# Four taps to a transpose instead of three in a two-block deformable-convolution kernel

## What is computed

```python
acc = acc + wgt[:, None] * g          # four corners of the bilinear sample, per tap
z = jnp.einsum('bckhw,ock->bohw', cols, w.reshape(O, C, 9))
...
x = x + L0(_gn(x))                    # one deformable convolution, relu
x = x + L1(_gn(x))                    # two of them, batch norm and gelu, own residual
```

## Time and profile before

| | us |
|---|---|
| median of 3 runs | 6690.79 (6690.13 to 6698.08) |
| the profiled execution, first to last instruction | 6690.3 |
| PE busy | 6000.0 (90%) |
| PE loading weights | 4792.9 (72%) |
| DVE busy | 4534.0 (68%) |
| POOL busy | 4608.7 (69%) |
| ACT busy | 2208.6 (33%) |

### The profile page before, as it was taken

How to read it: one execution, slowest core, us unless ns; L and a number is a source line. 1 busy time by engine, 2 the same in 40 slices (tenths; PEclk the granted TensorE clock), 3 DMA queues, 4 the chain that set the end, 5 groups by cost and what they waited for, 6 DMA issues and landing times. The chain is left out here.

```text
span 6690.3 us, 124828 instructions
## 1 busy us (share of the span) xinstructions
PE 6000.0 (90%) x48293; PEld 4792.9 (72%) x48293; DVE 4534.0 (68%) x8624; ACT 2208.6 (33%) x3376; POOL 4608.7 (69%) x4765
## 2 busy tenths in 40 slices
PE   6997998987988988998987998899989989998996
PEld 6886777766777767777765666677767777776775
DVE  6886776856777856777754555477667767676675
ACT  1222222232222222222322222244434444443442
POOL 0005777766777767777777777777777777777776
PEclk9998999988999988999987898899989999998998
DMA  5334344435343433444422332333333334333333
GB/s 148 99 99 116 100 112 114 113 88 141 100 112 104 119 82 108 109 111 107 110 79 75 82 78 73 98 87 84 84 94 95 91 80 103 91 88 86 87 84 77
DMA packets 505472, 653.42 MB, mean 98 GB/s; under 512 B 116137, under 2 KB 412121, under 8 KB 496985
## 3 DMA queue, kind: packets, MB, share of 16 engines
q0 software_dynamic: 152064, 311.73, 18.8%
q1 hardware_dynamic: 352856, 333.94, 17.7%
HBM read 599.16 MB, written 46.15 MB: 96 GB/s over the span
## 5 line engine op out<-in xcount | busy, mean ns | idle before, releaser
L895 POOL DMA_INDIRECT G<-table,IDX x4752 | 4594.6, 967 | 2036.7 <-issue 1932.9
L2282 DVE TENSOR_TENSOR ARENA<-ARENA,OUT 128x864 f32<-128x864 f32 x936 | 937.5, 1048 | 142.7 <-PE RED L1123 94.7
L1517 ACT ACTIVATE SAMP<-RED 96x384 f32<-96x384 f32 x688 | 335.2, 487 | 1889.8 <-PE RED L1335 824.9
L1123 PE MATMUL RED<-IDENT,ARENA 128*96 128x128 f32 x7344 | 876.1, 279 | 73.0 <-DVE ARENA L2282 73.0
L2085 DVE TENSOR_TENSOR G<-G,WPS 128x1152 f32<-128x1152 f32 x528 | 711.1, 1347 | 309.3 <-DMA G<-table,IDX 308.0
L1123 PEld LDWEIGHTS RED<-IDENT,ARENA 128*96 128x96 f32 x7344 | 816.5, 129 | 117.4 <-issue 114.3
L1316 PE MATMUL BTP<-PAD,ARENA 80*128 x2304 | 748.5, 448 | 56.8 <-DVE ARENA L2078 29.9
L1072 PE MATMUL OFF<-PAD,ARENA 128*54 128x128 f32 (+1 forms) x10944 | 748.5, 295 | 12.7 <-ACT PAD L1417 6.8
L1072 PEld LDWEIGHTS OFF<-PAD,ARENA 128*54 128x54 f32 (+1 forms) x10944 | 666.9, 134 | 112.9 <-issue 97.5
L1196 PE MATMUL BTP<-X 80*128 80x480 f32 x1248 | 648.7, 638 | 105.8 <-ACT X L1461 57.0
L1512 ACT ACTIVATE SAMP<-RED 96x384 f32<-96x384 f32 x528 | 257.3, 487 | 1450.4 <-PE RED L1138 733.7
(11 more groups left out here) (216 smaller groups left out, 7777.7 us busy)
## 6 DMA issues: line engine op xcount, KB each, us to landing
ARENA<-wtab SPq DMA_DIRECT2D x416, 400.0 KB
G<-table,IDX POOLq DMA_INDIRECT x4752
ARENA<-xo SPq DMA_DIRECT2D x96, 720.0 KB
X<-xo SPq DMA_DIRECT2D x80, 360.0 KB, 3.8
table<-TB SPq DMA_DIRECT2D x64, 384.0 KB, 2.5
X<-x SPq DMA_DIRECT2D x3, 3200.0 KB, 18.2
out<-X SPq DMA_DIRECT2D x20, 320.0 KB
wtab<-TB SPq DMA_DIRECT2D x16, 384.0 KB, 3.1
```

Of the source, the lines that this page charges most:

```text
L895: pool.indirect_dma_start(G[:, b, k, :], None, tables[seg.table], bass.IndirectOffsetOnAxis(ap=IDX[:, q, b * TAPS + k:b * TAPS + k + 1], a ...
L1123: last = nc.tensor.matmul(RED[b % 2][0:TPG * C, gr * 128:(gr + 1) * 128], PROD[gr][:, sft, :], IDENT[:, :], start=(sft == 0), stop=(sft == ...
L1517: nc.scalar.activation(SAMP[:, x], RED[x][0:TPG * C, 0:GROUPS * 128].rearrange("p (g n) -> p g n", g=GROUPS), ACT.Copy).then_inc(z.samp_re ...
L2282: nc.vector.tensor_tensor(out=PROD[gr].rearrange("p (dy dx) (j c) -> p j dy dx c", dy=3, j=TPG), in0=win.rearrange("p j dy (dx c) -> p j d ...
```

## The change

`TPB = 4`: taps go to transposes in blocks of four, four and one. A block of four fills 128 columns.

- Dense: `PROD` becomes one buffer for eight taps, nine shifts, and `PROD8` one for the ninth tap. PE makes 9 transposes for taps 0 to 3, 9 for taps 4 to 7, and 3 for the last tap: four shifts, one shift, four shifts at a time. These last leave four partial sums on the partitions, and the projection adds them, with the last tap's weights present four times in `WDCN`. 21 transposes a unit instead of 27.
- DVE still works dense taps by threes, but the third group is split in two taps (576 elements) and one (288). So PE's first block waits for two DVE instructions (`prod` counts 4 a unit now, 16 a tile) and DVE's second instruction waits for PE's second block of the unit before.
- Strips: 10, 10 and 3 transposes (23 instead of 30 a unit), DVE's instructions stay, one per tap.
- Gathered tiles: as many transposes as before, with 128, 128 and 32 columns instead of 96 each. Half strips stay at three groups, with their own weights `WHALF`.
- Start: `WDCN` is loaded by 24 DMAs and `WHALF` by one, all behind the two loads of `X`, where three DMAs stood ahead of them; PE waits for them before its first work (`norm`, k = 0). DVE clears both `RED` banks first.
- Smaller: ACT copies 128 instead of 96 partitions; `PRODS`, `OFFX`, `PXP` move.

```diff
-        PROD = [arena(5468 + 864 * i, 864).rearrange("p (s c) -> p s c", s=9) for i in range(GROUPS)]
+        PROD = arena(5468, 9 * 2 * TPB * C).rearrange("p (s k c) -> p s k c", s=9, k=2 * TPB)
+        PROD8 = arena(5468 + 9 * 2 * TPB * C, 9 * C).rearrange("p (s k c) -> p s k c", s=9, k=1)
...
-                sp.dma_start(WDCN[:, s], w_dcn[s]).then_inc(consts_loaded, 16)
             for h in range(HALVES):
                 load_x(h).then_inc(x_loaded, 16)
+            for s in (L0, C1, C2):
+                for k, n in ((0, 3), (3, 1), (4, 2), (6, 2)):
+                    at, src = k % TPB * C, k % TPG * C
+                    sp.dma_start(WDCN[at:at + n * C, s, k // TPB, :], w_dcn[s][src:src + n * C, k // TPG, :]).then_inc(wdcn_loaded, 16)
+                for r in range(TPB):
+                    sp.dma_start(WDCN[r * C:(r + 1) * C, s, 2, :], w_dcn[s][2 * C:3 * C, 2, :]).then_inc(wdcn_loaded, 16)
+            sp.dma_start(WHALF[:, :, :], w_dcn[C1]).then_inc(wdcn_loaded, 16)
...
+            def sum_window(red, gr):
+                if gr < GROUPS - 1:
+                    for sft in range(9):
+                        last = nc.tensor.matmul(red[:, gr * 128:(gr + 1) * 128], PROD[:, sft, TPB * gr:TPB * (gr + 1), :].rearrange("p k c -> p (k c)"),
+                                                IDENT[:, :], start=(sft == 0), stop=(sft == 8), is_transpose=True)
+                    return last
+                for sft, n in ((0, 4), (8, 1), (4, 4)):
+                    last = nc.tensor.matmul(red[0:n * C, gr * 128:(gr + 1) * 128], PROD8[:, sft:sft + n, 0, :].rearrange("p s c -> p (s c)"),
+                                            IDENT[:, :], start=(sft == 0), stop=(sft == 4), is_transpose=True)
+                return last
...
                 def norm(k, h, half, src, u=None, z=main):
                     pe.wait_ge(normed_s, k + 1)
                     pe.wait_ge(normed_v, k + 1)
+                    if k == 0:
+                        pe.wait_ge(wdcn_loaded, 16 * NWDCN)
...
                         for gr in range(GROUPS):
-                            pe.wait_ge(prod, 12 * step.i + 3 * b + gr + 1)
-                            for sft in range(9):
-                                last = nc.tensor.matmul(RED[b % 2][0:TPG * C, gr * 128:(gr + 1) * 128],
-                                                        PROD[gr][:, sft, :], IDENT[:, :],
-                                                        start=(sft == 0), stop=(sft == 8), is_transpose=True)
-                            last.then_inc(prod_used, 1)
+                            pe.wait_ge(prod, 16 * step.i + 4 * b + gr + 2)
+                            sum_window(RED[b % 2], gr).then_inc(prod_used, 1)
...
-                    pe.wait_ge(weighted, 36 * (now.s.first + now.k) + 9 * b + 3 * gr + 3)
+                    pe.wait_ge(weighted, 36 * (now.s.first + now.k) + 9 * b + min(TPB * (gr + 1), TAPS))
...
                 def weight_window(step, b, gr):
-                    dve.wait_ge(prod_used, step.wg + (GROUPS if step.drain and b == 0 else 3 * b + gr + 1))
+                    dve.wait_ge(prod_used, step.wg + (GROUPS if step.drain and b == 0 else 3 * b + min(gr + 1, 2)))
+                    if gr < GROUPS - 1:
+                        on.weight_taps(step, b, gr, 0, TPG, PROD[:, :, TPG * gr:TPG * (gr + 1), :])
+                        return
+                    on.weight_taps(step, b, gr, 0, 2, PROD[:, :, TPG * gr:TPG * gr + 2, :])
+                    dve.wait_ge(prod_used, step.wg + (GROUPS if step.drain and b == 0 else 3 * b + 3))
+                    on.weight_taps(step, b, gr, 2, 1, PROD8)
```

More of the change, by code:

```diff
@@ L13 @@
 TAPS, GROUPS, TPG = 9, 3, 3
+TPB = 4
 PW = W + 2
@@ L184, in build_program @@
         SHIFT = arena(7078, 1)
-        PXP = spare(1576, 256, 1)
+        PXP = ARENA[0:1, 6208:6464]
         IOTA = sb("IOTA", [128, WY])[:, :]
@@ L932, in _, with turn_taps, sum_rows @@
         def _(pe):
+            def turn_taps(red, b):
+                for gr in range(GROUPS):
+                    taps_ = SUM[:, b % 2, TPB * gr:min(TPB * (gr + 1), TAPS), :].rearrange("p k c -> p (k c)")
+                    last = nc.tensor.transpose(red[0:taps_.shape[1], gr * 128:(gr + 1) * 128], taps_, IDENT[:, :])
+                return last
[8 more added lines that the diff above has]
+                                            IDENT[:, :], start=(sft == 0), stop=(sft == 4), is_transpose=True)
+                return last
+            def sum_rows(red, gr):
+                if gr < GROUPS - 1:
+                    for w in range(WY):
+                        last = nc.tensor.matmul(red[:, gr * 128:(gr + 1) * 128], PRODS[gr][:, w, :],
+                                                IDENT[:, :], start=(w == 0), stop=(w == WY - 1), is_transpose=True)
+                    return last
+                for w, n in ((0, 4), (8, 2), (4, 4)):
+                    last = nc.tensor.matmul(red[0:n * C, gr * 128:(gr + 1) * 128], PRODS[gr][:, w:w + n, :].rearrange("p w c -> p (w c)"),
+                                            IDENT[:, :], start=(w == 0), stop=(w == 4), is_transpose=True)
+                return last
             class on:
@@ L1106, in consume @@
                         else:
[L1107 to L1111, removed]
+                            turn_taps(RED[b % 2], b).then_inc(z.reduced, 1)
                         if b == 2:
@@ L1150, in reduce_beside @@
                     for gr in range(GROUPS):
-                        pe.wait_ge(prod, 12 * dense.i + 3 * b + gr + 1)
-                        for sft in range(9):
-                            last = nc.tensor.matmul(RED[1][0:TPG * C, gr * 128:(gr + 1) * 128],
-                                                    PROD[gr][:, sft, :], IDENT[:, :],
-                                                    start=(sft == 0), stop=(sft == 8), is_transpose=True)
-                        last.then_inc(prod_used, 1)
+                        pe.wait_ge(prod, 16 * dense.i + 4 * b + gr + 2)
+                        sum_window(RED[1], gr).then_inc(prod_used, 1)
                 def project_pair(step, dense, b):
@@ L1322, in reduce @@
                         pe.wait_ge(main.samp_ready, unit(now, b, 1) + 1)
-                    pe.wait_ge(weighted, 36 * (now.s.first + now.k) + 9 * b + 3 * gr + 3)
-                    for w in range(WY):
-                        last = nc.tensor.matmul(RED[1][0:TPG * C, gr * 128:(gr + 1) * 128],
-                                                PRODS[gr][:, w, :], IDENT[:, :],
-                                                start=(w == 0), stop=(w == WY - 1), is_transpose=True)
-                    last.then_inc(prod_used, 1)
+                    pe.wait_ge(weighted, 36 * (now.s.first + now.k) + 9 * b + min(TPB * (gr + 1), TAPS))
+                    sum_rows(RED[1], gr).then_inc(prod_used, 1)
                 def turn_sums(now, b):
@@ L1333, in turn_sums @@
                     pe.wait_ge(main.samp_ready, unit(now, b, 0) + 1)
-                    for gr in range(GROUPS):
-                        last = nc.tensor.transpose(RED[0][0:TPG * C, gr * 128:(gr + 1) * 128],
-                                                   SUM[:, b % 2, TPG * gr:TPG * (gr + 1), :].rearrange("p k c -> p (k c)"),
-                                                   IDENT[:, :])
-                    last.then_inc(main.reduced, 1)
+                    turn_taps(RED[0], b).then_inc(main.reduced, 1)
                 def project_both(now, b):
@@ L2315, in check @@
                     nc.vector.tensor_scalar(FLAG[0:1, 0:1], CHK[0:1, 1:2], REACH, None, ALU.is_gt).then_inc(flag_ready, 1)
+            for red in RED:
+                nc.vector.memset(red[:, :], 0.0)
             nc.vector.memset(OFFS[:, :, :], 0.0)
```

68 lines of the change are left out of this document (42 added, 26 removed).

## The result

The changed kernel takes 6829.8 us (median of 4 runs, 6820.7 to 6840.7) where the kernel before, timed beside it, takes 6693.7. The ratio is 1.0205, 95% interval 1.0191 to 1.0220: **slower by about 2%**. The prediction was 6642 with a range of 6600 to 6690, faster. The profiled execution spans 6838.9 us, with PE busy 5955.9 us (before 6000.0), DVE 4568.6 (4534.0) and POOL 4640.9 (4608.7).

What follows compares the result with a forecast made beforehand. PE was taken to bound pair 0's dense tiles, POOL's gathers the rest, with some 78 us of POOL waits to win. 6690.3 - 28 + 9 - 30 + 0 = 6641.3, so 6642 us, range 6600 to 6690.

Steps and rivals of the forecast that it cites:

- The worth of a transpose: On PE, transposes of 128 loaded columns stand 0.109 us apart, like those of 96; upper bound 0.135.
- Rival 3: PE's transpose distance goes by loaded columns, 0.135 us for 128, so no PE time is saved: 6747 us, chance 0.08.
- The dense phase: The 26 dense tiles of pair 0, PE-bound: 1.1 us less a step, -28 us, bounds -62 and +17.
- The recurrence: Dense units, second block to second block through DVE and PE's first block: 15.4 us a step, 16.48 for before.
- the loop: Dense units: PE's second block, one DVE instruction with hand-over, PE's first block in series, 3.47 us.
- The start: PE's first work waits for 25 small DMAs behind X, starting at 53.3 us: +9 us, bounds 0 and +13.
- Gathered tiles, wider copies, moved buffers: 0: Gathered tiles and ACT's copies: as many transposes at the same distance, copy time by columns: 0 us, +-8.
- Dense tiles in convolution 1: Late tiles where POOL waits for DVE's sums: about 0.65 us gained per dense tile, -30 us, bounds 0 and -78.5.
- "-1.0 us" for an x tile: Convolution 1, mixed tiles: the end of an x tile comes 1.0 us earlier.
- "-0.35 net" for a d tile: Convolution 1, d tiles: a tighter loop gains 0.35 us, net of a first block waiting one more 0.97 us instruction.
- rival 1: Convolution 1's waits stay, from tiles behind the dense ones or a lower clock for an idler PE: 6672 us, chance 0.20.
- Strips: 0: Convolution 2's strips: 3 us less PE a round and a longer chain, all on slack: 0 us, -2 to +10.

Runs made afterwards that it cites:

- e3: Changed kernel with its 25 small weight loads moved behind the first tile's window loads, PE's wait for them to the first projection: 6810.9 us, ratio 1.0171.
- e1: Changed kernel with the gathered tiles' last tap projected over all 128 rows, zero weights below row 32: 6714.8 us, ratio 1.0031 to the kernel before.
- e2: Kernel before with gathered tiles' last group projected from 32 rows only, eighth and ninth tap left out: 6787.0 us, ratio 1.0143.
- e4: Changed kernel with the edits of e1 and e3 together: 6698.9 us, ratio 1.0007 to the kernel before.
- e5: e4 with the dense tiles of pairs 1 to 3 back to threes, 27 transposes a unit; pair 0 stays by fours: 6665.7 us, ratio 0.9959.

## Why the prediction was wrong, step by step

- **The worth of a transpose, right.** 0.109 us with 128 loaded columns, as taken from the one such load inside a block. Rival 3 (0.135, the distance by columns) is excluded. The rule of the Trainium skill named there (TensorE: Matmul & The Clock Gate, LDWEIGHTS) doesn't set the distance here, and the 81 ns of that page's section Back-to-back issue gap aren't reached.
- **The dense phase, right.** -28 forecast; 464 us from the end of the builds to the first gather, where 489 before, -25. The recurrence gave 4.42, 3.47, 3.6 and 3.9 us for the four units, 15.4 a step; measured are 4.50, 3.47, 3.55 and 4.01 from first block to first block, 15.5. The hand-over of 0.11 in the loop had no row of its own; the loop's 3.47 bears it out as a whole.
- **The start, right in kind, the term undersized.** +9 forecast, +13.4 measured (builds end at 70.58, before 57.16). The term that was too small is the price of a load: each of these took 0.5 us of the queue, where I had taken 0.36 from a `WDCN` load of the kernel before. In e3 they take 0.5 us at a later place as well, so the place behind `X` alone doesn't explain it; why they take more stays open. e3 gives the term back.
- **"Gathered tiles, wider copies, moved buffers: 0". This step failed**, by about 115 us. I counted transposes there and checked their distance, and did not follow the operand that they leave: with blocks of four, four and one, the projection of a gathered tile has a third group of one tap, 32 rows. The diff showed it (`k_in`), and my text speaks of projections only with dense tiles. e1 takes it out (-115), e2 puts it in (+93). None of my rivals held it. The wider copies in the same term did cost nothing: 489 ns each, where 487 before. The Trainium skill does: TensorEngine Tiling (Array Packing), Tiling Modes, says under its key properties that a change of the tiling mode drains the engine. The records agree: 0.20 us on each side of the 32-row matmul, where 0.11 stands between equal ones.
- **Dense tiles in convolution 1: wrong sign.** Forecast -30, with "-1.0 us" for an x tile and "-0.35 net" for a d tile. Measured with the 32-row matmul out: +32 in e1, +30 in e4. At the full clock the x tile did gain its 1.0 us; the d tile lost 0.28 where I had it gain. I took the loop's gain from a steady row of dense tiles and only subtracted one instruction. In a mixed stretch a tile starts with PE empty, so the first block's wait of two instructions (1.22 to 2.17 us) isn't covered by the tile ahead, and 17.4 us became 17.7. I had named the first block's wait and put it beside other work; the work was not there. The larger part is the granted clock (0.917 before, 0.906 in e1, 0.904 in e4 over convolution 1): it stood in my bounds and in rival 1 ("a PE that idles more is given a lower clock"), and the sum had no term for it. e5 gives both back.
- **Strips: 0, right.** In e1, with 3 us less of PE in each round, convolution 2 takes 2355.9 us against 2353.2. The tap that comes later fits into the slack.
- **Convolution 2 of the changed kernel, +45: source shown, path open.** Without the 32-row matmul (e1) it is 3, with it in the kernel before (e2) 17, so 32-row matmul and strips by fours together cost more than either. In pair 1 POOL waits 21 us for sums, in rounds with builds, where before 2. In pairs 0 and 2 it waits no more than before, but its gathers last longer, by 10 and 15 us in all. POOL's grouped lines of pair 2, before (5481:6082), after (5611:6227) and e1 (5502:6103), with the mean of a gather behind the comma:

```profile
L895 POOL DMA_INDIRECT G<-table,IDX x469 | 459.3, 979 | 142.9 <-issue 142.3 <-DVE SUM L2106 0.6
```
```profile
L911 POOL DMA_INDIRECT G<-table,IDX x468 | 473.9, 1013 | 142.7 <-issue 142.7
```
```profile
L919 POOL DMA_INDIRECT G<-table,IDX x469 | 458.9, 978 | 142.9 <-issue 142.9
```

In the changed kernel the long ones last up to 1.9 us (before 1.5), beside short DVE instructions on `G` and the indices, at the same places of each round. That DVE's instructions fall on other gathers once a round has another beat is my reading; it was not tested. My bound for such meetings was 8 us.
- **The clock: not the main cause, but a part.** e2 is slow at 0.935, e1 regains 115 us at 0.919, and in convolution 2 e1 regains 43 us at the same 0.94: the loss by the 32-row matmul is not the clock's. In the remaining 30 us of convolution 1 the clock is the larger part, as the table of steps has it; there rival 1 was right in kind.

The sum as it was: -25 and +13 ahead of the first gather, +113 in convolution 1 (81 of them gone in e1; the other 32 went when e5 made the mixed dense tiles by threes again), +45 in convolution 2 (43 gone in e1).

## What to carry to other kernels

When a change gives an operation a new shape, follow the result to every instruction that reads it: here a block of one tap saved nothing and made a 32-row matmul between 128-row ones, 0.6 us each time; padding with zero weights took 115 us away, placing it last 66. A gain measured in a steady row of equal tiles doesn't hold for the same tile between others: ask what the engine has to do while the first block waits. Here part of the work taken from PE came back as a lower granted clock, so compare steps at the same clock. And where a stretch isn't bound by the engine that gets faster, leave it as it was: the dense tiles of pair 0 by fours and those of the other pairs by threes beat both kernels.

## What the runs showed of the hardware

- A group of six float32 projections takes 1.09 us with equal row counts, 1.73 with one of 32 rows in the middle and 1.19 with it last. Before, the records of the two units lie between each other (starts at 868.65, 868.76, 868.79, 868.87 us), and 128-row and 96-row ones still do so in the changed kernel (688.821 and 688.828 us); across a 32-row one they don't.
- Transposes of 96 and of 128 columns start 0.11 us apart alike, at a granted clock of 1.00.
- The same dense tile alone takes 17.4 us in a stretch with a granted clock of 1.00 and 19.0 with 0.91. With the mixed dense tiles by fours PE is busy 84% of convolution 1 at a clock of 0.904 (e4), by threes 88% at 0.924 (e5).
- Behind two large loads the first four small ones hold SP's queue 14.9 us, each further one 0.5 us; issued from 62.5 us on (e3) they take some 0.5 us each too.
